# A Mamba scan on one core: two of ScalarE's router steps moved, and four of sixteen states scaled by TensorE

## The reference

```python
delta = softplus(dt_raw @ dt_proj_w.T + dt_proj_b)      # (8, 512, 256)
dA  = exp(delta * A)                                    # 16 states per channel
dBu = (delta * u) * B_ssm                               # B_ssm: (8, 512, 16)
h   = dA_t * h + dBu_t                                  # over the 512 steps
y_t = sum over the 16 states of h * C_t
```

## Time and profile before

| what | value |
|---|---|
| median of 3 runs | 1334.63 us (1329.22 to 1386.09) |
| profiled execution: its time, its span | 1332.58 us, 1330.8 us |
| scan stage: first scan starts, last scan starts | 158.8 us, 562.0 us |
| mean granted TensorE clock | 0.918 of 2.4 GHz |
| busy: TensorE, VectorE, ScalarE, GpSimd | 1073.6, 930.6, 882.5, 542.6 us |
| scan instruction, 128 x 1024 | x128, 2.28 us |
| product on GpSimd, 128 x 1024 | x128, 2.37 us |
| scale activation, 128 x 256 | x512, 495 ns each record |
| exp activation, 128 x 511 | x256, 709 ns each record |

### The profile page before, as it was taken

How to read it: one execution, slowest core, us unless ns; L and a number is a source line. 1 busy time by engine, 2 the same in 40 slices (tenths; PEclk the granted TensorE clock), 3 DMA queues, 4 the chain that set the end, 5 groups by cost and what they waited for, 6 DMA issues and landing times. The chain is left out here.

```text
span 1330.8 us, 24580 instructions
## 1 busy us (share of the span) xinstructions
PE 1073.6 (81%) x7230; PEld 737.2 (55%) x7230; DVE 930.6 (70%) x2003; ACT 882.5 (66%) x1835; POOL 542.6 (41%) x367
## 2 busy tenths in 40 slices
PE   1776499879778888764993999999999999991797
PEld 1333277668667777744991445544454545541796
DVE  5899589879788797734661767776775867673465
ACT  1777699989889899712761657564665657560574
POOL 0466488897988888831441000010101010011244
PEclk9888699999999898886995999998999999995899
DMA  3000133333453353203331000000000000001331
GB/s 85 2 3 2 41 93 91 88 89 97 122 167 123 105 168 114 74 32 89 92 96 49 17 1 1 17 17 1 16 0 18 0 16 1 17 18 44 91 88 50
DMA packets 50630, 74.36 MB, mean 56 GB/s; under 512 B 7352, under 2 KB 28605, under 8 KB 50529
## 3 DMA queue, kind: packets, MB, share of 16 engines
q1 hardware_dynamic: 41504, 51.09, 14.0%
q0 software_dynamic: 5568, 12.66, 2.7%
q10 hardware_dynamic: 3456, 9.46, 2.2%
HBM read 57.86 MB, written 16.24 MB: 56 GB/s over the span
## 5 line engine op out<-in xcount | busy, mean ns | idle before, releaser
L930 DVE TENSOR_TENSOR_SCAN h<-d_a,p_dbu 128x1024 f32<-128x1024 f32 x128 | 291.8, 2282 | 72.1 <-ACT d_a L728 62.0
L680 POOL TENSOR_TENSOR h<-h,c_rep 128x1024 f32<-128x1024 f32 x128 | 300.9, 2367 | 53.8 <-DVE h L930 52.5
L1850 ACT ACTIVATE at_probs<-at_scores,at_min 128x512 f32<-128x512 f32 x256 | 183.9, 722 | 136.0 <-DVE at_min L1960 88.0
L1960 DVE CUSTOM_DVE_ANT_0 at_scores<-at_p_scores,arena 128x512 f32<-128x512 f32 x256 | 174.5, 684 | 91.4 <-PE at_p_scores L1726 53.0
L720 ACT ACTIVATE b_du_T<-arena,b_T 128x256 f32<-128x256 f32 x512 | 216.8, 495 | 0.1
L813 PE MATMUL p_dbu<-ident,b_du_T 128*128 128x128 f32 x1024 | 176.1, 302 | 40.9 <-ACT b_du_T L720 40.8
L1208 POOL TENSOR_SCALAR r_row<-r_row 128x4 f32<-128x4 f32 x16 | 3.7, 231 | 474.7 <-DVEq L1124 474.7
L728 ACT ACTIVATE d_a<-arena,a_exp 128x511 f32<-128x511 f32 x256 | 169.1, 709 | 0.0
L813 PEld LDWEIGHTS p_dbu<-ident,b_du_T 128*128 128x128 f32 x1024 | 119.9, 150 | 86.7 <-issue 52.0
L1733 PEld LDWEIGHTS at_p_probs_T<-ident,at_probs 128*128 128x128 f32 x1024 | 112.7, 142 | 93.2 <-issue 71.0
L1733 PE MATMUL at_p_probs_T<-ident,at_probs 128*128 128x128 f32 x1024 | 159.1, 283 | 6.2 <-ACT at_probs L1850 5.9
(11 more groups left out here) (220 smaller groups left out, 1532.5 us busy)
## 6 DMA issues: line engine op xcount, KB each, us to landing
c_rep<-c_rows SPq DMA_DIRECT2D x128, 256.0 KB, 3.4
f_row<-expert_rows SPq DMA_DIRECT2D x78, 129.0 KB
arena<-in_w_all ACTq DMA_DIRECT2D x8, 578.0 KB
arena<-bias_by_distance ACTq DMA_DIRECT2D x8, 448.0 KB
x_tok<-in_x SPq DMA_DIRECT2D x4, 512.0 KB, 5.6
x_tok<-x_between SPq DMA_DIRECT2D x8, 256.0 KB, 2.9
expert_rows<-f_pad SPq DMA_DIRECT2D x10, 129.0 KB, 3.1
expert_rows<-f_pad ACTq DMA_DIRECT2D x8, 129.0 KB, 3.4
```

The source lines that it names most:

```text
L680: nc.gpsimd.tensor_tensor(h[:, n % HS, :, :], h[:, n % HS, :, :], cc, ALU.mult).then_inc(prod_done, 1)
L930: nc.vector.tensor_tensor_scan(h[:, n % HS, :, :].rearrange("p c t -> p (c t)"), da[:, s % 2, :, :].rearrange("p c t -> p (c t)"), p_dbu[: ...
L1850: nc.scalar.activation(pr[:, s % 2, :], sc[:, s % 2, :], ACT.Exp, scale=-1.0, bias=mn[:, s % 2:s % 2 + 1]).then_inc(probs_ready, 1)
L1960: V.tensor_tensor_reduce(sc[:, s % 2, :], psc[:, s % SCB, :], band[:, hd, w0:w0 + T], 1.0, 3.0e38, ALU.add, ALU.min, mn[:, s % 2:s % 2 + 1 ...
```

## The change

In `mamba_scan`, `act_rstd` goes from before to behind the scalings of state 11, and `act_rows` from state 13 to state 15. In this router (`in_psum`) `act_rows` waits for `added` in place of `ln_ready`. In states 1, 3, 11 and 15 ScalarE multiplies the identity (128 x 128) by B, which gives a diagonal of B for each 128 tokens, in place of du (128 x 256); and TensorE's spread multiplies the turned du by that diagonal with true matmuls (still eight in the loops) in place of transposing the scaled du.

```diff
+    DIAG = (1, 3, 11, 15)
...
                 for j in range(TPB):
-                    nc.scalar.activation(b_du[:, s % SR, j, :], du_T(b, j), ACT.Copy,
+                    src, width = (k.ident[:], P) if s in DIAG else (du_T(b, j), DI)
+                    nc.scalar.activation(b_du[:, s % SR, j, 0:width], src, ACT.Copy,
                                          scale=bT[:, one(b), j, s:s + 1].squeeze(1)).then_inc(scaled, 1)
...
-                if s == 11 and not after_scale:
+                if s == 11 and after_scale:
                     rt.act_rstd(act, b)
-                elif s == 13 and after_scale:
-                    rt.act_rows(act, b)
                 elif s == 14 and after_scale:
                     rt.act_turned(act, b)
+                elif s == 15 and after_scale:
+                    rt.act_rows(act, b)
...
                     for ch in range(NC):
-                        mm = nc.tensor.transpose(p_dbu[:, s % 2, ch, j * P:(j + 1) * P],
-                                                 b_du[:, s % SR, j, ch * P:(ch + 1) * P], k.ident[:])
+                        dst = p_dbu[:, s % 2, ch, j * P:(j + 1) * P]
+                        if s in DIAG:
+                            mm = nc.tensor.matmul(dst, du_T(b, j)[:, ch * P:(ch + 1) * P], b_du[:, s % SR, j, 0:P],
+                                                  start=True, stop=True)
+                        else:
+                            mm = nc.tensor.transpose(dst, b_du[:, s % SR, j, ch * P:(ch + 1) * P], k.ident[:])
...
     def act_rows(self, act, b):
         self.rows_out(act, b)
-        act.wait_ge(self.ln_ready, 1 + b)
+        if self.in_psum:
+            act.wait_ge(*self.x_there(b))
+        else:
+            act.wait_ge(self.ln_ready, 1 + b)
```

## The result

| | before | after |
|---|---|---|
| median of 12 runs | 1333.43 us (1329.22 to 1386.09) | 1324.57 us (1321.74 to 1327.37) |
| ratio, 95% interval | 1 | 0.9937 [0.9926, 0.9949] |
| span of the profiled execution | 1330.8 us | 1319.9 us |
| last gate of the scan stage starts (VectorE) | 567.96 us | 559.33 us |
| from there to the end | 762.8 us | 760.6 us |

The account below looks back on a forecast made before the run. Bound: GpSimd's chain from scan 6 to the router's transposes, no engine by itself. Gains of 1.6, 2.7, 6.5 and 1.5 sum to 12.3 us: 1332.58 becomes 1320.3, with 2.05 for the median 1322 us; range 1304 to 1336.

Parts of the forecast that it names:

- rival 2: TensorE's clock: a long low stretch in every batch, 5.1 us gained, time 1330 us; chance 0.17.
- GpSimd's chain as the bound: Scan stage: the chain from scan 6 to the router's transposes, 23.35 us, holds neither ScalarE nor anything the diff touches.
- act_rstd and act_rows: ScalarE, states 11 to 15: the moves start exps 14 2.57 us earlier; act_rows costs its 0.54 us in state 15.
- The diagonals on ScalarE: ScalarE's scalings: 128 columns cost 0.294 us, saving 0.43 us per state and 1.71 us per batch.
- The diagonals on TensorE: TensorE's spread of a diagonal state takes 1.77 us instead of 0.87 at full clock; 3.5 with the clock low.
- Batches 0, 1 and 7: Scan stage: gains of 1.6 us up to the gate of batch 1, 2.7 in batch 1, 1.5 in batch 7.
- batches 2 to 6: Scan stage, long low-clock stretches in batches 2, 5 and 6: 3 x 0.36 + 2 x 2.7 = 6.5 us gained.
- The price of a long stretch: TensorE at 1.2 GHz for 10 us behind its pause: scan 3 comes later, 0.36 us of gain left per batch.
- rival 1: TensorE's clock doesn't fall, or only briefly: 19.3 us gained, time 1315 us; chance 0.22.
- Rival 3: All work saved arrives because GpSimd's chain starts earlier, down to its own 46.4 us: gain 38, time 1297; chance 0.08.

Follow-up runs that it names:

- Experiment 1: The changed kernel without the diagonals, act_rstd and act_rows in their new places: 1320.36 us, 0.9908 of the kernel before.
- experiment 2: The kernel before with diagonals in states 1, 3, 11 and 15 and nothing moved: 1338.28 us, 1.005 of the kernel before.
- experiment 3: The changed kernel with GpSimd's router rows before product 10 in place of 11: 1301.05 us (0.9765) with the diagonals, 1307.84 us (0.9822) without.

## Why the prediction was right

The forecast was 1322 us by the median then known, the change 12.3 us less than the kernel before; measured were 8.4 us by the ratio and 8.6 in the scan stage. That lies halfway between the forecast's own sum and that of rival 2 (5.1 us), so the time alone can't tell the two apart; the parts do.

- **GpSimd's chain as the bound:** right, and shown by the run that moved only GpSimd's rows. The wait of ScalarE went to the place that was named, before act_turned: 3.1 us forecast, 2.9 to 3.7 measured. From a gate to the next act_turned it was 35.82 us and is 33.16, or some 33.6 where the router's transposes themselves run at the low clock; forecast was a gain of 2.57.
- **act_rstd and act_rows:** right. Experiment 1 has the 0.54 of act_rows in the gate to the hundredth.
- **The diagonals on ScalarE:** right, 0.293 us against 0.294. The Trainium skill (ScalarE: Activation LUTs, What ACT_TABLE_LOAD costs) gives 186 ns and 0.833 ns per column, 93 for a scale per partition, and 93 of overlap back to back. For 128 columns that is an estimate of 0.293 us, and the trace agrees.
- **The diagonals on TensorE:** 1.87 us against 1.77 at the high clock, 3.46 against 3.5 at the low one. That they gain almost nothing at the high clock with state 3 among them was right too (16.26 for 16.21; the forecast was 0.1 less than before).
- **Batches 0, 1 and 7:** 1.5, 2.6 and 1.4 us against 1.6, 2.7 and 1.5.
- **The term that was mis-sized** is that of batches 2 to 6: 6.5 us forecast, 3.1 measured (-0.2, +2.3, -0.4, +0.7, +0.7). The price of a long stretch was too low: 0.36 us of gain left was forecast, and 10.5 us of it turned the gain into a loss (-0.2 and -0.4). In batch 4 the spread of state 15 ended 7.7 us behind exps 14 (393.16), where 7.6 was forecast, but scan 3 came 19.5 behind it for 18.7. The forecast names only VectorE's scans in between; TensorE's spread of state 3 and the sum of state 15, which can't start before scan 1 is through, end 0.87 us after VectorE is free.
- **Luck** is in where the stretches fell. Batches 2, 5 and 6 were to be long and 3 and 4 short. Batch 4 became long, and 5 and 6 came down to 7 us, so the errors nearly cancel: with stretches as assumed and the gains measured for each kind, the term is an estimate of 3.6 us (3 x -0.34 + 2 x 2.33), against the 3.1 measured. The periods were 49.7 us for a short stretch (49.3 forecast), and 51.3 and 52.5 to 52.6 for longer ones (51.6 forecast).
- **Rivals:** rival 1, with the clock high, put at 19.3 us, is the run with the pause filled, whose stage is 15.6 us shorter. Batches 2 to 6 gained 13.3 us for 13.5; missing are 2.4 us in batch 1, which the filling costs, and 1.0 in batch 7. Rival 2, all stretches long, is near what happened: four of five were 7 us or more. Rival 3 said that GpSimd could start earlier; it could not by itself, but moved by hand it came to 46.3 us per batch, its own work of 46.4.

What stays open is what decides between a stretch of 3.5 and one of 10.5 us. The same kernel has both, in batches that do the same work.

## What to carry to other kernels

When an engine stands still, follow the wait to the chain that has no gap, here GpSimd's, and move that: one product's place there gave 1.7% beside the 0.6% of the whole change, somewhat more than half of it by the shorter chain and the rest by the clock that no longer fell. One place further was worse, because another wait then stood in front. Work taken off the engine that waits becomes a longer wait (experiment 2), and only pays once the chain is off the path (experiment 3). Work put on TensorE right behind a pause must be priced at the low clock too; if it doesn't fit there, shorten the pause or put the work elsewhere, and not into the step that the next engine waits for.

## What the runs showed of the hardware

- In batches 2 to 6 of the changed kernel TensorE's clock fell to 1.2 GHz in each pause of 3.7 to 4.0 us or within about a microsecond behind it, and stayed there 3.5 to 10.5 us, although TensorE was busy without a gap behind the pause. With 32 transposes of the identity in the pause it stayed at 2.4 GHz in batches 1 to 6, and also with the pause cut to between 1.4 and 1.7 us.
- A low stretch is cheap or dear by what stands in it: with eight instructions per spread 10.5 us of it cost at most 0.5 us, with sixteen in two of the states up to 2.6 us.
- Transposes alone held the clock: in batch 0, from 190 to 210 us before the change, TensorE did nothing else and was granted 1.00. The Trainium skill (TensorE: Matmul & The Clock Gate, Part 4: PE-mode transpose) says that the high clock doesn't engage for transposes; the trace disagrees so far as holding it goes. Whether transposes alone would also raise it, no run shows.
